# A routing stage in which the threshold search uses one matrix product a round and the first choice is read from the logits

## The reference

```python
cap = int(math.ceil(CF * N / E))                    # N = 8192 tokens, E = 8, cap = 1229
probs = jax.nn.softmax(x @ Wr + br, axis=-1)
gates, ids = jax.lax.top_k(probs, K)                # K = 2
...
order = jnp.lexsort((-flat_g, flat_ids))            # by expert, then by gate, largest first
...
valid = rank < cap                                  # an expert keeps its `cap` largest gates
...
xg = x[disp_tok].reshape(E, cap, Dm)
h = jax.nn.silu(jnp.einsum('ecd,edh->ech', xg, W1) + b1[:, None, :])
out = jnp.einsum('ech,ehd->ecd', h, W2) + b2[:, None, :]
gated = out * disp_g.reshape(E, cap, 1)
y = jnp.zeros((N, Dm), x.dtype).at[disp_tok].add(gated.reshape(E * cap, Dm))
```

## Time and profile before

| | us |
|---|---|
| median of 3 runs | 954.77 |
| lowest and highest run | 954.52, 955.15 |
| the profiled execution | 954.1 |
| its span | 952.4 |
| mean granted PE clock in it | 0.835 of full speed |

### The profile page before, as it was taken

The page is one execution under the profiler, slowest core; times in us unless marked ns, Lnnn a source line. Parts: engine busy times, 40 slices in busy tenths (PEclk is TensorE's granted clock), DMA queues, the critical chain, the costliest instruction groups (busy, mean ns, idle before and its releaser), DMA issues. The chain is left out here.

```text
span 952.4 us, 15550 instructions
## 1 busy us (share of the span) xinstructions
PE 702.2 (74%) x4187; PEld 559.7 (59%) x4187; DVE 640.4 (67%) x2281; ACT 484.3 (51%) x1243; POOL 464.0 (49%) x590
## 2 busy tenths in 40 slices
PE   7457999999999993999898334275677867787600
PEld 3225777777777762989898224243566756676500
DVE  7656999999999954799898576793223222322387
ACT  4754566676666654878685224162222222222356
POOL 7502666676666762243333500004666666666462
PEclk8876999999999995999999555556978889888955
DMA  8920000000000006000000075003122212221197
GB/s 216 365 88 1 1 1 1 2 1 1 2 1 1 1 2 177 1 2 2 2 0 2 0 113 67 0 0 79 45 67 65 68 44 66 64 69 42 45 304 216
DMA packets 73233, 52.96 MB, mean 56 GB/s; under 512 B 11744, under 2 KB 67048, under 8 KB 72896
## 3 DMA queue, kind: packets, MB, share of 16 engines
q1 hardware_dynamic: 67312, 41.61, 16.5%
q0 software_dynamic: 5120, 10.37, 4.2%
q10 hardware_dynamic: 720, 0.05, 0.1%
HBM read 28.04 MB, written 24.18 MB: 55 GB/s over the span
## 5 line engine op out<-in xcount | busy, mean ns | idle before, releaser
L817 DVE SCALAR_TENSOR_TENSOR s_cv<-s_pU,tap_w,s_cv 128x256 f32<-128x256 f32 x384 | 159.6, 477 | 20.0 <-ACT s_cv L761 19.6
L1834 ACT ACTIVATE e_h<-e_pH,e_b 128x256 f32<-128x256 f32 x160 | 65.3, 472 | 166.7 <-remote 105.7
L1776 POOL DMA_INDIRECT e_xg<-token_rows,token_of x80 | 82.0, 1025 | 127.6 <-issue 127.6
L1810 PE MATMUL e_pH<-e_xgT,e_w 128*128 128x256 f32 x320 | 93.3, 443 | 51.2 <-issue 50.5
L1783 POOL DMA_INDIRECT choice_rows<-e_yo,choice_of x80 | 80.5, 1006 | 63.0 <-DVE e_yo L1879 39.6
L1810 PEld LDWEIGHTS e_pH<-e_xgT,e_w 128*128 128x128 f32 x320 | 67.3, 221 | 65.5 <-issue 54.8
L1820 PE MATMUL e_pO<-e_w,e_h 128*128 128x128 f32 x640 | 87.1, 287 | 6.1 <-issue 5.4
L1820 PEld LDWEIGHTS e_pO<-e_w,e_h 128*128 128x128 f32 x640 | 81.7, 204 | 8.9 <-issue 8.9
L637 POOL TENSOR_TENSOR s_xa<-s_xt,arena 128x512 f32<-128x512 f32 x32 | 34.4, 1075 | 103.2 <-ACT s_xt L779 103.2
L1872 DVE TENSOR_TENSOR e_ysum<-e_pO,e_b 128x256 f32<-128x256 f32 x40 | 17.0, 425 | 95.3 <-PE e_pO L1820 44.7
L666 PE MATMUL s_pU<-arena,w_in 128*128 128x262 f32 x256 | 72.3, 407 | 11.7 <-DVE s_cv L817 8.4
(11 more groups left out here) (285 smaller groups left out, 1862.8 us busy)
## 6 DMA issues: line engine op xcount, KB each, us to landing
choice_rows<-zrow SPq DMA_DIRECT2D x16, 512.0 KB, 7.2
arena<-choice_rows SPq DMA_DIRECT2D x32, 256.0 KB, 5.1
token_rows<-arena SPq DMA_DIRECT2D x8, 520.0 KB, 12.6
n_x<-in_L_attn_x_dram SPq DMA_DIRECT2D x8, 512.0 KB, 7.6
arena<-in_L_attn_x_dram SPq DMA_DIRECT2D x8, 512.0 KB, 4.6
e_w<-in_L_ffn_W_dram SPq DMA_DIRECT2D x16, 256.0 KB
out_dram<-arena SPq DMA_DIRECT2D x16, 256.0 KB, 4.4
decay_rows<-arena SPq DMA_DIRECT2D x2, 1024.0 KB, 4.7
```

Of the source, the lines that this page charges most:

```text
L817: v.scalar_tensor_tensor(out=by_tile(cv[:, p % 2, m, :]), in0=columns(m)[:, :, tap:tap + P], scalar=tap_w[:, m, tap:tap + 1], in1=by_tile( ...
L1776: g.indirect_dma_start(xg[:, n % RING, i, :], None, table, bass.IndirectOffsetOnAxis(ap=token_of[:, G * n + i:G * n + i + 1], axis=0), bou ...
L1810: ins = pe.matmul(pH[n % 2][half_][:, ROWS * c:ROWS * (c + 1)], we1[:, expert(n), P * f:P * (f + 1)], xgT[:, n % 2, :], start=True, stop=True)
L1834: ins = a.activation(hb[:, n % 2, f, :], pH[n % 2][half_][:, ROWS * c:ROWS * (c + 1)], ACT.Silu, bias=be1[:, expert(n), f:f + 1])
```

## The change

- Search: ACT's sums of signs and DVE's counts go into one tile `cnt` of four columns, and one product with `same_e` adds up all of them. The products with `half_e` and `half` are gone, and so are these two tiles. `decide` compares each column with its own threshold from a tile `enough`: the capacity 1229 for the counts, and 2 * 1229 - 8192 for the sums of signs. It becomes a `scalar_tensor_tensor` with an accumulator in place of a `tensor_scalar` with one.
- Choice: the maximum, the subtraction and the first equality test read the logits and stand ahead of the wait for POOL's constants. The marks of the first choice (`first_of`) are made while ACT makes the exponentials. The maximum and the equality test on the probabilities are dropped for the first choice; its probability is the reciprocal of the sum. The operation that subtracted 1 from the gates of experts not chosen is dropped.
- Waits: PE has three waits ahead of its one product. DVE's wait for the constants now stands between the first equality test and the product with `rev`.

```diff
--- before.py
+++ after.py
@@ -1346,18 +1346,18 @@
             hi, lo, fine = (sbt("r_" + n, [P, 512]) for n in ("hi", "lo", "fine"))
             signs = sbt("r_signs", [P, 2, 512], BF16)
             cand, later, found = (sbt("r_" + n, [P, 4]) for n in ("cand", "later", "found"))
-            cnt_v, cnt_a, half = (sbt("r_" + n, [P, 2]) for n in ("cnt_v", "cnt_a", "half"))
+            cnt, enough = sbt("r_cnt", [P, 4]), sbt("r_enough", [P, 4])
             reach, digit = sbt("r_reach", [P, 4]), sbt("r_digit", [P, 1])
             ends = sbt("r_ends", [P, 2])
             offs = sbt("r_offs", [P, 7])
             base = sbt("r_base", [P, 1])
-            same_e, half_e = sbt("r_same_e", [P, P]), sbt("r_half_e", [P, P])
+            same_e = sbt("r_same_e", [P, P])
             before = sbt("r_before", [P, P])
             pG, pC, pI = pst("r_pG"), pst("r_pC"), pst("r_pI")
             s_c, s_v, s_ex, s_exp, s_q, s_pg, s_tot, s_end, s_off, s_pos, s_pi, s_go = (
                 sem("r_" + n) for n in ("c", "v", "ex", "exp", "q", "pg", "tot", "end", "off", "pos", "pi", "go"))
-            s_digit, s_cand, s_later, s_found, s_cnt_v, s_cnt_a, s_hi, s_low_i, s_lo, s_fine, s_half = (
-                sem("r_" + n) for n in ("digit", "cand", "later", "found", "cnt_v", "cnt_a", "hi", "low_i", "lo", "fine", "half_"))
+            s_digit, s_cand, s_later, s_found, s_cnt_v, s_cnt_a, s_hi, s_low_i, s_lo, s_fine = (
+                sem("r_" + n) for n in ("digit", "cand", "later", "found", "cnt_v", "cnt_a", "hi", "low_i", "lo", "fine"))
             LOW = 7
             COARSE, FINE = 10, 4
             ROUNDS = COARSE + FINE
@@ -1424,9 +1424,8 @@
                     g.affine_select(out=base[:, :], in_=base[:, :], compare_op=ALU.is_ge, fill=REGION * e - 1.0,
                                     base=16 * e - 1, pattern=[[0, 1]], channel_multiplier=-1).then_inc(s_c, 1)
                     g.wait_ge(s_c, n + 1 + e)
-                g.memset(half[:, :], 512.0)
-                g.wait_ge(s_c, n + E)
-                g.tensor_scalar(half_e[:, :], same_e[:, :], 0.5, None, ALU.mult).then_inc(s_half, 1)
+                g.memset(enough[:, 0:2], float(CAP))
+                g.memset(enough[:, 2:4], float(2 * CAP - TOKENS))
                 for i in range(ROUNDS):
                     for o in range(4):
                         g.memset(starts[:, i, o:o + 1], start_of[i][o])
@@ -1446,7 +1445,7 @@
             @block.scalar
             def _(a):
                 a.wait_ge(s_ex, 1)
-                a.activation(pr[:, :, :], eq[:, :, :], ACT.Exp).then_inc(s_exp, 1)
+                a.activation(pr[:, :, :], gt_[:, :, :], ACT.Exp).then_inc(s_exp, 1)
                 a.wait_ge(s_low_i, 1)
                 a.activation(lo[:, :], lo_i[:, :], ACT.Copy, scale=2.0 ** -LOW).then_inc(s_lo, 1)
 
@@ -1455,7 +1454,7 @@
                     a.wait_ge(*((s_hi, 1) if i < COARSE else (s_fine, 1)))
                     src = hi if i < COARSE else fine
                     for o in range(2):
-                        ins = a.activation(signs[:, o, :], src[:, :], ACT.Sign, bias=cand[:, 2 + o:3 + o], accum_out=cnt_a[:, o:o + 1])
+                        ins = a.activation(signs[:, o, :], src[:, :], ACT.Sign, bias=cand[:, 2 + o:3 + o], accum_out=cnt[:, 2 + o:3 + o])
                     ins.then_inc(s_cnt_a, 1)
                 for i in range(ROUNDS):
                     counted_above(i)
@@ -1473,14 +1472,11 @@
                     pe.wait_ge(s_q, q + 1)
                     pe.transpose(pG[:, P * q:P * (q + 1)], gq[:, q, :], ident[:, :]).then_inc(s_pg, 1)
                 pe.wait_ge(s_c, 15)
-                pe.wait_ge(s_half, 1)
                 for i in range(ROUNDS):
                     need(pe, s_digit, i, 1)
-                    pe.matmul(pC[:, 2:4], half_e[:, :], half[:, :], start=True, stop=False)
                     need(pe, s_cnt_a, i)
-                    pe.matmul(pC[:, 2:4], half_e[:, :], cnt_a[:, :], start=False, stop=True)
                     need(pe, s_cnt_v, i)
-                    pe.matmul(pC[:, 0:2], same_e[:, :], cnt_v[:, :], start=True, stop=True).then_inc(s_tot, 1)
+                    pe.matmul(pC[:, 0:4], same_e[:, :], cnt[:, :], start=True, stop=True).then_inc(s_tot, 1)
                 pe.wait_ge(s_end, 2)
                 pe.matmul(pC[:, 0:2], before[:, :], ends[:, :], start=True, stop=True)
                 pe.matmul(pC[:, 2:4], same_e[:, :], ends[:, :], start=True, stop=True).then_inc(s_off, 1)
@@ -1512,30 +1508,29 @@
                     ins.then_inc(s_v, 1)
                     v.wait_ge(s_v, chain[0])
 
-                def best(src, top, first, weight):
-
-                    link(v.tensor_reduce(top, src, AX.X, ALU.max))
-                    link(v.tensor_tensor(eq[:, :, :], src, over_e(top), ALU.is_equal))
+                def first_of(first, weight):
+
                     link(v.tensor_tensor(w[:, :, :], eq[:, :, :], rev[:, :].unsqueeze(1).broadcast_to([P, TILES, E]), ALU.mult))
                     link(v.tensor_reduce(weight, w[:, :, :], AX.X, ALU.max))
                     link(v.tensor_tensor(first, w[:, :, :], over_e(weight), ALU.is_equal))
+
+                link(v.tensor_reduce(mx[:, :], logits[:, :, :], AX.X, ALU.max))
+                v.tensor_tensor(gt_[:, :, :], logits[:, :, :], over_e(mx[:, :]), ALU.subtract).then_inc(s_ex, 1)
+                link(v.tensor_tensor(eq[:, :, :], logits[:, :, :], over_e(mx[:, :]), ALU.is_equal))
                 v.wait_ge(s_c, 5)
-
-                link(v.tensor_reduce(mx[:, :], logits[:, :, :], AX.X, ALU.max))
-                v.tensor_tensor(eq[:, :, :], logits[:, :, :], over_e(mx[:, :]), ALU.subtract).then_inc(s_ex, 1)
+                first_of(f1[:, :, :], wm[:, :])
                 v.wait_ge(s_exp, 1)
                 link(v.tensor_reduce(sm[:, :], pr[:, :, :], AX.X, ALU.add))
-                link(v.reciprocal(mx[:, :], sm[:, :]))
-                link(v.tensor_tensor(pr[:, :, :], pr[:, :, :], over_e(mx[:, :]), ALU.mult))
-
-                best(pr[:, :, :], m1[:, :], f1[:, :, :], wm[:, :])
+                link(v.reciprocal(m1[:, :], sm[:, :]))
+                link(v.tensor_tensor(pr[:, :, :], pr[:, :, :], over_e(m1[:, :]), ALU.mult))
+
                 link(v.scalar_tensor_tensor(out=gt_[:, :, :], in0=f1[:, :, :], scalar=-2.0, in1=pr[:, :, :], op0=ALU.mult, op1=ALU.add))
-                best(gt_[:, :, :], m2[:, :], f2[:, :, :], wm[:, :])
+                link(v.tensor_reduce(m2[:, :], gt_[:, :, :], AX.X, ALU.max))
+                link(v.tensor_tensor(eq[:, :, :], gt_[:, :, :], over_e(m2[:, :]), ALU.is_equal))
+                first_of(f2[:, :, :], wm[:, :])
                 link(v.tensor_tensor(selq[:, :, :], f1[:, :, :], f2[:, :, :], ALU.add))
                 link(v.tensor_tensor(gates[:, :, :], pr[:, :, :], selq[:, :, :], ALU.mult))
 
-                link(v.scalar_tensor_tensor(out=gates[:, :, :], in0=selq[:, :, :], scalar=-1.0, in1=gates[:, :, :],
-                                            op0=ALU.add, op1=ALU.add))
                 for q in range(4):
                     v.tensor_copy(gq[:, q, :].rearrange("p (e b h) -> p e b h", e=E, h=2), by_chunk(gates[:, :, :], q)).then_inc(s_q, 1)
                 v.tensor_copy(rows[:, :, D], m1[:, :]).then_inc(s_go, 1)
@@ -1557,7 +1552,7 @@
                     src = hi if i < COARSE else fine
                     for o in range(2):
                         ins = v.tensor_scalar((above, same)[o][:, :], src[:, :], cand[:, o:o + 1], 0.0, ALU.is_ge, ALU.add,
-                                              accum_out=cnt_v[:, o:o + 1])
+                                              accum_out=cnt[:, o:o + 1])
                     ins.then_inc(s_cnt_v, 1)
 
                 def proceed(i):
@@ -1572,8 +1567,8 @@
 
                 def decide(i):
                     need(v, s_tot, i)
-                    v.tensor_scalar(reach[:, :], pC[:, 0:4], float(CAP), 0.0, ALU.is_ge, ALU.add,
-                                    accum_out=digit[:, :]).then_inc(s_digit, 1)
+                    v.scalar_tensor_tensor(out=reach[:, :], in0=pC[:, 0:4], scalar=1.0, in1=enough[:, :], op0=ALU.mult, op1=ALU.is_ge,
+                                           accum_out=digit[:, :]).then_inc(s_digit, 1)
                     need(v, s_digit, i)
 
                 def next_cand(i):
```

## The result

| | before | after |
|---|---|---|
| median of 4 runs, us | 954.96 | 944.19 |
| lowest run, us | 954.52 | 941.10 |
| the profiled execution, us | 954.1 | 945.9 |
| its span, us | 952.4 | 944.2 |

One run of the kernel before took 3254.91 us; it counts in the median (954.77 without it) and not in the ratio. The ratio of the runs is 0.9885, with a 95% interval of 0.9851 to 0.9920. The kernel is about 1.15% faster, 11.0 us by the ratio (7.6 to 14.2 by its interval), where 9.4 were forecast. Measured again beside the kernels built on it, the same change gave a median of 945.97 against 957.16, a ratio of 0.9898 (0.9881 to 0.9914), so 9.8 us.

What follows compares the result with a forecast made beforehand. The prediction took the routing stage to be bound by chains of short handoffs between engines. Choice 4.2 plus search 5.2 made 9.4 us, so 954.8 became 945.4 us, with 943.2 to 948.3 for eight in ten.

Steps and rivals of the forecast that it cites:

- The start of the choice: In the choice: DVE starts before POOL's constants and drops operations, so the copies come at 550.93, saving 4.2 us.
- The three parts of this saving: In the choice: early maximum and subtraction with the exponentials' wait 2.11, maximum and equality on probabilities 1.45, last subtraction 0.72.
- The cover: In the choice: three DVE operations run beside POOL's constants without delaying them; nothing charged, at most 1.4 us.
- Rival 2: In the choice: POOL's constants come late by DVE's two-tensor operations, 1.4 us, giving 946.8 us; 12%.
- The round: In the search: ACT's end to the decision falls from 1.10 to 0.73 us, 0.37 a round, 5.2 us over 14.
- the late wait: In each search round: ACT's wait, ending last of three ahead of PE's product, costs 0.07 us more.
- DVE's own late wait: In the choice: the product with `rev`, behind two waits, starts 0.13 us after POOL's last constant.
- Rival 1: In the search: the single product is no shorter behind ACT than the pair, giving 951.6 us; 4%.
- Rival 3: In the search: PE's late wait costs nothing, 1.0 us more saved, giving 944.4 us; 8%.
- Rival 4: In the expert stage: it gives the gain back, over 9.4 us, at about 955.5 us; 3%.
- Rival 5: In the expert stage: it moves a few microseconds either way without undoing the gain, 941.5 to 950 us; 10%.
- one slow step: In the expert stage: a step's eight products on PE's lower clock level, sized 2.0 us, used to widen the range downward.

Runs made afterwards that it cites:

- e8: The changed kernel with its one product made twice each round, both behind ACT's wait; search 45.62 us against 39.64, kernel 951.75 us in one run.
- e4: The changed kernel with ACT's wait put first of the three ahead of PE's product; search 39.38 us, kernel 945.28 us, ratio 0.9888 to the kernel before.
- e3: The changed kernel with two extra hidden products each round, restoring PE's old 42 search products; 945.58 us, ratio 0.9888 to the kernel before.
- e5: The changed kernel with POOL making `rev` first and DVE waiting for it alone before the first marks; choice 13.11 us, kernel 946.17 us in one run.

## Why the prediction was right

**The start of the choice.** Forecast: first maximum at about 537.5, product at 540.9, copies at 550.9, against the old span's zero. The changed kernel's routing stage began 0.66 us earlier (table load 536.76 against 537.42), and with that taken off all three hold: 537.46, 540.90, 551.03. The saving was 4.1 us where 4.2 were forecast. The 0.1 is the product held up by a select. The three parts of this saving (2.11, 1.45 and 0.72 in the forecast) were not run one by one; only their sum is measured.

**The cover.** The constants did not come late by the operations beside them: POOL's part from the table load to the last constant took 3.37 us (540.13 - 536.76) against 3.38 before. Rival 2 did not come. The mechanism behind it exists, though, and I set it aside too easily: the earlier trace rows compare memsets, which read nothing, and I let them speak for POOL as a whole, while the old trace held a select beside a subtraction at 541.69. The price was 0.12 us, since the selects stand beside the chain: a select that began while an operation of it ran lost time itself, and only one select had begun just ahead of such an operation and held it up.

**The round.** Forecast 0.37, measured 0.41 a round, so 5.7 us and not 5.2. The mechanism was right, and e8 shows it alone. The term that was mis-sized is the late wait: I took 0.07 from the placing loop, and it cost 0.02, as e4 and e8 both show. The isolated product took 0.63 from the load to the decision and not 0.62. The 0.07 was the difference between two loops with different products, and no run changed the waits of the placing loop, so what part of its 0.11 us they cost stays open. DVE's own late wait cost what was forecast to within 0.02 (0.11 against 0.13 in the earlier trace rows). `decide` cost nothing more. Rival 1, a product that isn't shorter, is out. Rival 3, a wait that is free, is out by only 0.02 a round, and the measured wait lies nearer to it than to the forecast's 0.07.

**The other side.** Rival 4 did not come: the expert stage did not answer to the list (e3) or to the moment of its start, as far as its scatter lets one see. Rival 5, a stage that moves by a few microseconds, is true of every kernel here, the one before included. I had argued from three runs that agreed within 0.7 us that the stage is steady. Sixteen later runs of the kernel before on one chip lie between 951.27 and 959.20, so three runs were too few for that argument, and the range held because it had been widened for one slow step: the forecast's own range, 944.4 to 946.2, missed the median by 0.2. That the median of four runs fell into the wider range of 943.2 to 948.3 was in part luck, since single runs of the changed kernel lie between 941.10 and 949.00.

**The sum.** For the profiled execution 944.7 was forecast and 945.9 measured: 954.1 - 4.1 - 5.7 = 944.3, and 1.6 more from stages that the change doesn't touch (0.65 less to the logits, 1.5 more in the expert stage, 0.75 more in the tail). That is scatter by the profiles above. The median, 944.19 against 945.4, lies on the other side of the forecast by as much. What is shown is the 9.8 us of the two stages; the 11.0 of the first comparison and the 9.8 of the second both agree with it within their intervals.

## What to carry to other kernels

In a chain of handoffs, count only what stands behind the wait that ends last: of the two products that the change removes in each round one was hidden and worth nothing, and the other was worth its 0.43 us fourteen times. A wait for a batch of constants should be moved as late as possible and ask for no more than the next operation reads: in e5 that gave 1.44 us more. Where runs scatter by more than an edit is worth, compare stages between fixed events of the profiles, which here repeat to 0.01 us, and ask for more than three runs before calling any stage steady.

## What the runs showed of the hardware

- POOL's affine selects and DVE's operations on two SBUF tensors hold each other up: a select of 0.29 to 0.34 us took 0.63 to 0.70 when it began beside one, and the DVE operation 0.77 to 0.81 in place of 0.69 when a select had begun 0.03 to 0.08 us before it. Memsets and iotas of POOL ran beside the same operations at their usual pace.
- Of several waits ahead of a PE product, the order matters a little: with the one that ends last standing first, the waiting DVE operation began 0.67 us after ACT's end, and 0.69 with it in second place; over 14 rounds that was 0.26 us.
- Placed right behind another one, an fp32 product of 128 x 128 weights with four columns costs 0.43 us at a granted clock of 0.50 (e8, 5.98 us over 14 rounds).
